# Cross-attention scores from two 64-row halves of TensorE instead of zero-padded 128-row products

## The reference

```python
q = x @ Wq; k = context @ Wk; v = context @ Wv      # 16 heads of 64, x: 256 rows, context: 77 rows
sim = jnp.einsum('bhid,bhjd->bhij', q, k) * SCALE
attn = jax.nn.softmax(sim, axis=-1)
out = jnp.einsum('bhij,bhjd->bhid', attn, v)
return out @ Wo + bo
```

## Time and profile before

| | us |
|---|---|
| median of 3 runs (1518.70 to 1519.46) | 1518.88 |
| the profiled execution | 1519.74 |
| its span, first to last instruction | 1518.0 |
| TensorE busy in the span | 1266.3 |
| VectorE busy | 945.8 |
| GpSimd busy | 628.5 |
| ScalarE busy | 555.1 |

### The profile page before, as it was taken

The page is one execution under the profiler, slowest core; times in us unless marked ns, Lnnn a source line. Parts: engine busy times, 40 slices in busy tenths (PEclk is TensorE's granted clock), DMA queues, the critical chain, the costliest instruction groups (busy, mean ns, idle before and its releaser), DMA issues. The chain is left out here.

```text
span 1518.0 us, 24131 instructions
## 1 busy us (share of the span) xinstructions
PE 1266.3 (83%) x8285; PEld 1072.1 (71%) x8285; DVE 945.8 (62%) x1563; ACT 555.1 (37%) x970; POOL 628.5 (41%) x475
## 2 busy tenths in 40 slices
PE   5304998887899888799888799999289999999996
PEld 3202677666676776566766677877279999999996
DVE  4795446757537567544586733333377888888884
ACT  1001222322313233231332333334156666666662
POOL 5443036453207536212745422111325555555542
PEclk9755999999999999899999899999689999999998
DMA  8101010101101100100012201000256676666660
GB/s 178 31 0 35 3 23 1 23 23 29 25 1 23 24 1 23 44 10 11 13 23 47 60 23 24 15 1 15 77 171 233 232 236 231 212 224 206 231 203 6
DMA packets 69816, 113.50 MB, mean 75 GB/s; under 512 B 22135, under 2 KB 56649, under 8 KB 63824
## 3 DMA queue, kind: packets, MB, share of 16 engines
q1 hardware_dynamic: 53776, 91.11, 19.7%
q0 software_dynamic: 15936, 21.07, 4.9%
HBM read 102.96 MB, written 14.64 MB: 77 GB/s over the span
## 5 line engine op out<-in xcount | busy, mean ns | idle before, releaser
L1516 PE MATMUL psH<-xhigh,whigh 128*128 128x256 f32 x736 | 209.4, 285 | 7.9 <-DVE wlow L1364 6.5
L1516 PE MATMUL psH<-xlow,whigh 128*128 128x256 f32 x736 | 207.1, 281 | 0.0
L1516 PE MATMUL psH<-xhigh,wlow 128*128 128x256 f32 x736 | 207.0, 281 | 0.0
L349 POOL TENSOR_TENSOR ve<-mv,eps 128x2 f32<-128x2 f32 (+1 forms) x36 | 9.4, 262 | 430.3 <-DVE mv L802 366.1
L1364 DVE TENSOR_TENSOR wlow<-staged,whigh 128x2048 fp32r<-128x2048 f32 x69 | 158.8, 2302 | 0.0
L1516 PEld LDWEIGHTS psH<-xhigh,whigh 128*128 128x128 f32 x736 | 141.4, 192 | 8.6 <-issue 6.7
L1002 PE MATMUL psA<-qT,kT 128*77 128x256 f32 x512 | 145.1, 382 | 0.0
L1022 PE MATMUL psD<-vo,pT 128*128 128x128 f32 x1024 | 133.7, 278 | 12.9 <-DVE o L774 12.6
L1022 PEld LDWEIGHTS psD<-vo,pT 128*128 128x128 f32 x1024 | 124.7, 193 | 25.1 <-issue 16.0
L1433 ACT ACTIVATE whigh<-staged 128x2048 fp32r<-128x2048 f32 x69 | 132.3, 1919 | 26.5 <-PEq L140 15.6
L1516 PEld LDWEIGHTS psH<-xlow,whigh 128*128 128x128 f32 x736 | 140.4, 191 | 0.0
(11 more groups left out here) (192 smaller groups left out, 2822.4 us busy)
## 6 DMA issues: line engine op xcount, KB each, us to landing
staged<-in_L_ffn_w SPq DMA_DIRECT2D x69, 1024.0 KB, 5.0
tokens<-out_rows POOLq DMA_DIRECT2D x32, 256.0 KB, 6.9
xb<-in_x SPq DMA_DIRECT2D x32, 128.0 KB
b2s<-in_L_ffn_b SPq DMA_DIRECT2D x23, 128.0 KB
xw<-in_x SPq DMA_DIRECT2D x4, 512.0 KB
xw<-in_x SPq DMA_DIRECT2D x16, 64.0 KB
wq<-in_L_xattn_Wq SPq DMA_DIRECT2D x1, 1024.0 KB, 12.5
wo<-in_L_xattn_Wo SPq DMA_DIRECT2D x1, 1024.0 KB, 12.4
```

Of the source, the lines that this page charges most:

```text
L1516: ins = mm(psH[:, q % 2 * PAIR + c, part, :], lhs, rhs, start=i == 0, stop=i == len(passes) - 1)
```

## The change

Each score product now uses only the 64 partitions of its head: `kT[rows, ...]` with `qT[rows, ...]`, rows 0 to 63 for even heads and 64 to 127 for odd heads. The two products of a pair stand next to each other in TensorE's order and write to different banks: bank S{2w} now gets the even heads 4w and 4w+2, bank S{2w+1} the odd heads 4w+1 and 4w+3. The two shifts (128 rows, unchanged in kind) follow the two products. `values` finds its probabilities in the new places. The first pair of products, which stood on both sides of `scores_for_max(3)`, now stands behind it. The number of products, shifts, exponentials, banks and semaphore increments is the same.

```diff
-                    def score_products(u, m):
-                        ps = freeA(f"S{u}", j, b)
-                        mm(ps[0:CTX, m * N:(m + 1) * N], kT[:, u, m, :], qT[:, u, :], start=True, stop=False)
-                    def score_shift(u, m):
-                        ps = psA[:, A(f"S{u}", j, b)[1], :]
-                        ins = mm(ps[0:CTX, m * N:(m + 1) * N], head_row[:, 2 * u + m, :], nmT[:], start=False, stop=True)
-                        if m == 1:
-                            ins.then_inc(a_full, 1)
-                    def scores(u):
+                    def score_products(w, i):
                         for m in range(2):
-                            score_products(u, m)
-                            score_shift(u, m)
+                            ps = freeA(f"S{2 * w + m}", j, b)
+                            rows = slice(m * D2, (m + 1) * D2)
+                            mm(ps[0:CTX, i * N:(i + 1) * N], kT[rows, 2 * w + i, m, :], qT[rows, 2 * w + i, :],
+                               start=True, stop=False)
+                    def score_shifts(w, i):
+                        for m in range(2):
+                            ps = psA[:, A(f"S{2 * w + m}", j, b)[1], :]
+                            ins = mm(ps[0:CTX, i * N:(i + 1) * N], head_row[:, 4 * w + 2 * i + m, :], nmT[:],
+                                     start=False, stop=True)
+                            if i == 1:
+                                ins.then_inc(a_full, 1)
+                    def scores(w):
+                        for i in range(2):
+                            score_products(w, i)
+                            score_shifts(w, i)
...
-                                     pT[:, (2 * w + m // 2) % 4, (m % 2) * N + t * P:(m % 2) * N + (t + 1) * P],
+                                     pT[:, (2 * w + m % 2) % 4, (m // 2) * N + t * P:(m // 2) * N + (t + 1) * P],
...
+                    scores_for_max(3)
                     score_products(0, 0)
-                    scores_for_max(3)
-                    score_products(1, 0)
...
-                    for u in range(2):
-                        score_shift(u, 0)
-                        score_products(u, 1)
-                        score_shift(u, 1)
-                    scores(2)
-                    scores(3)
+                    score_shifts(0, 0)
+                    score_products(0, 1)
+                    score_shifts(0, 1)
+                    scores(1)
...
                         if v in (1, 3):
-                            scores(v + 3)
-                            scores(v + 4)
+                            scores(v // 2 + 2)
```

## The result

The changed kernel takes 1508.47 us (median of 20 runs, 1502.55 to 1517.62) against 1519.31 us for the kernel before (20 runs, 1513.80 to 1523.51). The ratio is 0.9934, 95% interval 0.9922 to 0.9946; by it the kernel is 10.0 us faster, between 8.2 and 11.9. The forecast was 1525.9 us, slower. The profiled execution of the changed kernel is its fastest run, 1502.55 us, with a span of 1500.8 us, so differences of whole spans are too large by some 6 us; what follows is read from starts and from single sequences.

What follows compares the result with a forecast made beforehand. TensorE was taken to bound the last turn and `b` = 0. Pairs 0.109 us longer, counted 49 times, gave +5.3 us, the clock +1.7, ACT zero: +7.0 on the 1518.88 median, 1525.9 us; range 1509 to 1541.

Steps and rivals of the forecast that it cites:

- The bound: Whole sequences: TensorE sets the end in the last turn and at `b` = 0; elsewhere it waits for VectorE.
- Slots of a pair: Score products: a pair's four records take three slots, 0.65 us; with shifts 0.865 us against 1.082, 0.217 gained.
- both products wholly side by side: Rival on score products: a pair's products take 0.433 us; 1513.4 us, or 1500.1 without switch cost; chance 0.06.
- The switch: Between split products and whole-row shifts, twice a pair: 0.163 us each, bounds zero and 0.196, break-even 0.108.
- the whole tail of 0.163 us: At a switch: next load and product wait until the last result is out, 0.163 us after its slot.
- the 0.033 of a start from standstill: At a switch: a start without preloaded weights adds 0.033 us, read from L1007 behind a wait, 0.30 against 0.27.
- the switch is cheap: Rival on row-mode changes: only 0.033 us each, a pair takes 0.931 us; 1511.6 us, 1508.7 if free; chance 0.22.
- Where pairs count: Exposed pairs in the last turn and at `b` = 0: losses count 49 times, gains 40; 49 x 0.109 = +5.3 us.
- The shadow: Behind `scores_for_max(3)`: the first pair ends at 1041.69, before the second NM transpose at 1041.89, so only 7 pairs are exposed.
- The clock: Maxima's stretch holds 0.2 us less work, so one more of seven sequences may fall to half clock: +1.7 us.
- The rival had the lower level far too cheap: Rival in the scores: half-idle rows lower the clock, 1.7 us in each of seven sequences, 11.9 us; 1536.1; chance 0.12.
- ACT at zero cost: Exponentials: the second ends about 0.6 us later, but values come late enough that nothing waits; cost zero.

Runs made afterwards that it cites:

- the run on the same rows: Changed kernel with both products of a pair on rows 0 to 63, even heads' scores replacing the odd heads'; ratio 1.0213 to the kernel before.
- The run with each product alone: Changed kernel with all products on rows 0 to 63, each followed at once by its own shift except in the first pair; ratio 1.0695.
- the one without switches in a pair: Changed kernel with the shifts on 64 rows too, negated maxima and head_row laid out to fit; 1501.94 us, ratio 0.9897.
- The change in the last turn alone: Changed kernel's order everywhere, but products on 64 rows only in the last turn, all rows in the first three; ratio 0.996.
- The repeat: The changed kernel unaltered, measured again on one chip with a later run; 1508.50 us, ratio 0.9941.
- the two kernels that save more: Changed kernel with four products then four shifts (1504.40 us, ratio 0.9926), and changed kernel with shifts on 64 rows too (1501.94 us, ratio 0.9897).

## Why the prediction was wrong

**The bound.** Right: in the last turn and at `b` = 0 TensorE sets the end, and the last turn's sequences moved by 7 pairs (1.0 us measured against 7 x 0.147).

**Slots of a pair: the step that failed.** "I take three, 0.65 us", since "the even head's second record must follow its first" and starts are in program order. The records show two and two: 0.50 us to the end of the second slot with the slow start, 0.433 without. The third slot that I counted, 0.216 us a pair, isn't there, and with it went the sign. The rival "both products wholly side by side" had this right, with a chance of only 0.06. The first records of a pair start together, and in the run on the same rows none did, so one of each product runs at a time. The weight loads of the trace show the same order: each product's first load waits for its bank, and in the changed kernel both such loads start (1027.302 and 1027.308) before the other two (1027.367 and 1027.374), while on the same rows they alternate (981.428, 981.494, 981.709, 981.925). Whether the program already holds the records in that order or TensorE puts them so, no run here shows. The Trainium skill ("TensorE: Matmul & The Clock Gate", Part 3, The mechanism) has matmuls on different row groups start some 4 ns apart. The trace agrees in the main: the first records of the pair start at 1027.303 and 1027.310, 7 ns apart. Of the two sums given with it the shorter was the right one.

**The switch.** Its bounds held: 0.326 us for two was taken, 0.28 measured. But the wait is not for the whole tail of 0.163 us: the first shift starts at 1027.89, while the records before it last until 1027.96. The array is idle for some 0.095 us at each change, and the slower first slot adds 0.06 for a product and 0.03 for a shift. I had read the 0.033 of a start from standstill off a shift; a product's costs twice that. The idle times are even under the 0.1 us that I had named as a sign of being wrong. The run with each product alone adds 0.27 for one more round trip, and the one without switches in a pair has none. The Trainium skill ("TensorEngine Tiling (Array Packing)", Key Properties) says that a change of the tiling mode drains TensorE; the gaps here, and their absence where only the half changes, agree.

The pair: 0.433 + 0.216 + 0.28 = 0.93 us against 1.191 forecast, so 0.147 gained and not 0.109 lost. The rival "the switch is cheap" gives the pair 0.931 us as well, by three slots and nearly free switches. That is a coincidence: the records show two slots and dearer switches.

**Where pairs count.** 40 x 0.147 = 5.9, and 3 x 0.5 before norm1 = 1.5: 7.4 us. The change in the last turn alone agrees with its share. The repeat holds 7.4 (6 to 12 us); the first comparison, 8.2 to 11.9, lies above it.

Two things are missing from that sum. I had no gain at `b` = 3, but there each of the six windows of the two profiles of the changed kernel is shorter than before's, by 0.5 to 1.8 us; the chain behind this was not followed. At `b` = 2 four of the six are 0.8 us longer (51.5 us with a clock of 0.97 against 50.7 with 0.99 to 1.00). At `b` = 1 four of six are as before, 54.3 us with a clock of 0.94, the other two 51.1 with 1.00 and 53.5 with 0.92. So a better clock over the whole execution is not what goes beyond 7.4 us: the median of an execution's mean clock is 0.925 in the changed kernel and 0.931 or 0.932 in the kernel before. The profiled execution, with 0.931, is the exception and the fastest.

**The shadow** of the maxima held: TensorE's wait before the second transpose is 0.20 us, where it was 0.21.

**The clock.** The place was wrong, the direction right. Of the last four sequences none has a lower clock in one profile and one in another, as before; but over the whole execution the mean clock is lower, as said above, and lower still in the two kernels that save more. The rival had the lower level far too cheap where products run on half the rows alone: the times are 14 us beyond the sum in one run and some 70 in another, of which at most 61 are the clock's in the sequences summed above.

**ACT at zero cost.** Right for the changed kernel; at 0.54 us a pair the values wait 0.28 us for it.

## What to carry to other kernels

Count record slots only after the starts: products of fp32 on different halves of the rows ran wholly side by side here, which made two 0.43 us products one, while each change between split and whole rows took 0.13 to 0.16 us. So put as much as possible between two changes, best by putting the neighbours of the small products on split rows as well. Products on half the rows that had no partner were worse here than zero-padded ones: they saved nothing, paid the changes, and the clock stayed at its lower level for longer. And a saving counted in slots came back only in part in the two fastest kernels, which also had a lower mean granted clock; how much of the missing part is the clock's was not separated.

## What the runs showed of the hardware that was not expected

- Two fp32 products on rows 0 to 63 and 64 to 127, two records each, took two slots of 0.216 us; on the same rows four.
- Behind the maxima's idle time the granted clock stayed at 0.50 for 10.2 us of work without a gap where products used 64 rows one after another. In the kernel before it was back at 1.00 after 3.4 us of such work.
- The mean granted clock of an execution was 0.929 to 0.934 with all rows and 0.917 to 0.924 in the two fastest kernels.
- A change between split and whole rows left the array idle for some 0.095 us; between fp32 and bf16 on split rows there was no gap.
- Two bf16 shifts of 256 columns on different halves took one slot of 0.11 us.
